# First attention in two PSUM banks, second attention's scores in two banks by turns

## The reference, cut to what matters

```python
x = x + tanh(g_xattn[0]) * xattn0(layernorm(x), ctx, mask)   # A: 4 heads of 64, one K/V head, rotary, masked, 120 context rows
x = x + tanh(g_ffn[0])   * ffn0(layernorm(x))                # F: gated SiLU, 704 wide, FP4 quantise-dequantise of inputs and weights
x = x + tanh(g_xattn[1]) * xattn1(layernorm(x), ctx, ctx)    # B: 16 heads of 16, biases, 120 context rows
x = x + tanh(g_ffn[1])   * moe(layernorm(x))                 # R, M: 8 experts, top 2, 1024 wide
```

## Time and profile before

| | us |
|---|---|
| median of 3 runs | 1848.67 |
| lowest, highest | 1848.36, 1865.61 |
| the profiled execution's own time | 1838.81 |
| span of its instructions | 1837.2 |
| TensorE busy | 1540.0 |
| VectorE busy | 1121.2 |
| ScalarE busy | 886.8 |
| GpSimd busy | 591.9 |

### The profile page before, as it was taken

One profiled execution on the slowest core, in us unless ns is written; L12 is line 12 of the kernel. 1 busy time (PEld: TensorE's weight loads), 2 busy tenths in 40 slices (PEclk: granted clock), 3 DMA queues, 4 the chain that ended last, 5 costly groups with the idle time before them and its releaser, 6 DMA issues.

```text
span 1837.2 us, 35831 instructions
## 1 busy us (share of the span) xinstructions
PE 1540.0 (84%) x12221; PEld 1239.6 (67%) x12222; DVE 1121.2 (61%) x2782; ACT 886.8 (48%) x2169; POOL 591.9 (32%) x704
## 2 busy tenths in 40 slices
PE   2334899999998999899989877649999999999994
PEld 1223577667766767676766554438888888888884
DVE  4657678877787778787777552234444444444442
ACT  1111466656666656665655453214444544445542
POOL 0002324333434243334332421023443434434432
PEclk9557999999999999999999896569999999999998
DMA  5002211222022202221122000157213232232224
GB/s 172 11 0 78 81 57 37 92 92 84 10 92 92 91 9 87 92 93 43 51 84 84 7 7 12 48 160 239 39 32 100 34 103 34 33 101 34 29 34 114
DMA packets 63088, 123.60 MB, mean 67 GB/s; under 512 B 13890, under 2 KB 51899, under 8 KB 58811
## 3 DMA queue, kind: packets, MB, share of 16 engines
q1 hardware_dynamic: 45675, 102.75, 16.3%
q0 software_dynamic: 17312, 19.56, 6.6%
HBM read 78.63 MB, written 48.04 MB: 69 GB/s over the span
## 4 chain that ended last, share of the span: by engine, by line
PE 76%; DVE 9%; ACT 7%; issue 3%; DMA 2%; POOL 1%; SPq 0%; ACTq 0%; DVEq 0%; POOLq 0%
PE bank L1247 17%; PE bank L1249 16%; PE bank L1248 16%; PE bank L1319 9%; PE bank L1343 7%; PE bank L1332 3%; ACT b_ex L687 2%; DVE b_mn L1008 2%; ACT b_q L747 1%; PE bank L1359 1%; PE bank L1521 1%; ACT r_z L670 1%; PE bank L1467 1%; PE bank L1411 1%; PE bank L1431 1%
## 5 line engine op out<-in xcount | busy, mean ns | idle before, releaser
L1247 PE MATMUL bank<-split_room,wm 128*128 128x256 f16 x1152 | 314.9, 273 | 8.3 <-issue 6.9
L1249 PE MATMUL bank<-split_room,wm 128*128 128x256 f16 x1152 | 314.8, 273 | 0.0
L1248 PE MATMUL bank<-split_room,wm 128*128 128x256 f16 x1152 | 314.7, 273 | 0.0
L1224 DVE SCALAR_TENSOR_TENSOR split_room<-bank,b12e,split_room 128x256 f32<-128x256 f32 x288 | 138.3, 484 | 266.0 <-ACT split_room L798 258.2
L798 ACT ACTIVATE split_room<-bank,b12e 128x256 f32<-128x256 f32 x288 | 134.3, 470 | 196.0 <-PE bank L1249 192.6
L687 ACT ACTIVATE b_ex<-bank,b_mn 128x120 f32<-128x120 f32 x512 | 143.6, 373 | 117.5 <-DVE b_mn L1008 116.4
L1319 PE MATMUL bank<-b_k,b_q 128*128 128x480 f32 x256 | 140.8, 634 | 39.0 <-ACT b_ex L687 23.3
L1343 PEld LDWEIGHTS bank<-b_v,b_pt 120*128 120x128 f32 x1024 | 137.9, 204 | 36.0 <-issue 31.7
L643 POOL DMA_INDIRECT acc<-split_room,m_cur x72 | 115.3, 1602 | 131.7 <-ACT split_room L812 104.3
L1247 PE MATMUL bank<-wm,split_room 128*128 128x256 f16 x576 | 157.0, 273 | 0.0
L1249 PE MATMUL bank<-wm,split_room 128*128 128x256 f16 x576 | 157.0, 273 | 0.0
(11 more groups left out here) (358 smaller groups left out, 3859.7 us busy)
## 6 DMA issues: line engine op xcount, KB each, us to landing
split_room<-in_L_ffn_W SPq DMA_DIRECT2D x48, 512.0 KB, 8.4
wsplit<-split_room SPq DMA_DIRECT2D x16, 1536.0 KB, 6.5
wm<-wsplit SPq DMA_DIRECT2D x16, 1536.0 KB, 8.9
acc<-x SPq DMA_DIRECT2D x17, 256.0 KB, 2.1
xin<-in_x SPq DMA_DIRECT2D x16, 256.0 KB
rows<-r_row SPq DMA_DIRECT2D x16, 256.0 KB, 8.2
ct<-in_ctx SPq DMA_DIRECT2D x16, 120.0 KB
cb<-in_ctx SPq DMA_DIRECT2D x16, 120.0 KB, 2.1
```

What stands on the lines that cost most here:

```text
L1224: dve.scalar_tensor_tensor(m_h[:, c % 3], bank[c % 4][:, TILE:2 * TILE], b12e[:, p, 1, c:c + 1], m_s[:, c % 2], ALU.add, ALU.mult).then_in ...
L1247: pe.matmul(o, lh, rh, start=start, stop=False)
L1248: pe.matmul(o, ll, rh, start=False, stop=False)
L1249: return pe.matmul(o, lh, rl, start=False, stop=stop)
```

## The change

- B's scores alternate between bank 3 and bank 2. Scores of round k wait for the exponentials of round k - 2, and the exponentials of round k from 2 on wait for the transposes of round k - 2, whose buffer they overwrite.
- A uses banks 0 and 1 alone. A.q is cut in two pieces, A.q0 and A.q1, one per pair of heads, each with both rotary halves in one bank (0 and 1); A.q1 waits until VectorE has read A.kv's results from bank 1. A.rot becomes A.rk (keys and values) and A.r0, A.r1 (queries, 256 wide each). A's values go into bank 0 for the first half of the queries and bank 1 for the second; the first wait until all of A's exponentials are done.
- B.q writes banks 3 and 2, and waits for the ranks no more; the first values of B wait for them instead.
- All five lists are new. The number and shape of products on TensorE are the same.

```diff
@@ -355,19 +355,19 @@
 
         RA, RB = NT, NT * (H1 // QUAD)
         ORDER = {
-            "SP": ("A.load/-1 B.out/3 B.load/0 W/0 R.rank/3").split(),
-            "POOL": ("B.ln/2 R.ln/3 A.ln/-1 F.p0/1 W0/0 W1/0 F.p1/1 F.ln/0 W2/0 F.p/0 R.scatter/3").split(),
-            "ACT": ("F.gu3/2 B.k/3 B.q/3 B.s0/3 B.s1/3 B.t0/3 F.ht0/2 B.s2/3 B.t1/3 B.t2/3 B.s3/3 F.ht1/2 A.s0/0 B.t3/3 "
-                "B.s4/3 B.s5/3 B.t4/3 F.z/1 A.s1/0 A.t0/0 B.s6/3 B.t5/3 A.t1/0 B.s7/3 B.t6/3 B.t7/3 F.t/1 A.ot/0 B.ot/3 "
-                "F.gu0/1 B.z/2 F.gu1/1 R.z/3 R.t/3 A.z/-1 B.ct/2 B.zt/2 F.gu2/1 A.t/-1 R.logit/3").split(),
-            "DVE": ("B.s0/3 F.q1b/2 B.v/3 B.s1/3 F.q1c/2 B.s2/3 F.ht0/2 A.rot/0 B.s3/3 A.s0/0 B.s4/3 F.ht1/2 F.ln/1 B.s5/3 "
-                "W0/1 A.s1/0 W1/1 B.s6/3 B.p3/3 F.q/1 B.s7/3 F.d1/2 A.p0/0 A.p1/0 F.t/1 B.p7/3 B.ln/2 A.ot/0 B.ot/3 W2/1 "
-                "B.out/3 F.gu0/1 R.ln/3 A.out/0 A.ln/-1 F.gu1/1 R.t/3 F.q0a/1 F.gu2/1 B.ct/2 R.logit/3 B.zt/2 R.rank/3 "
-                "A.t/-1 F.gu3/1 F.q0b/1 F.q1a/1 F.q0c/1").split(),
-            "PE": ("F.ht1/2 A.s0/0 B.t3/3 B.s4/3 B.p2/3 A.s1/0 A.t0/0 B.s5/3 B.t4/3 F.d0/2 B.s6/3 B.p3/3 F.d1/2 B.p4/3 "
-                "B.t5/3 B.s7/3 A.t1/0 A.p0/0 B.t6/3 B.p5/3 A.p1/0 B.t7/3 F.t/1 B.p6/3 B.p7/3 A.ot/0 B.ot/3 F.gu0/1 "
-                "B.out/3 A.out/0 F.gu1/1 B.ct/2 B.zt/2 R.t/3 F.gu2/1 R.logit/3 A.t/-1 F.gu3/1 R.rank/3 B.k/2 B.q/2 "
-                "A.kv/-1 B.s0/2 B.v/2 A.q/-1 B.s1/2 B.t0/2 F.ht0/1 B.s2/2 B.p0/2 B.t1/2 B.t2/2 B.s3/2 B.p1/2").split(),
+            "SP": ("A.load/-1 W/1 B.out/3 B.load/0 R.rank/3").split(),
+            "POOL": ("B.ln/2 A.ln/-1 R.ln/3 W0/1 F.p0/1 F.p1/1 W1/1 F.ln/0 F.p/0 W2/1 R.scatter/3").split(),
+            "ACT": ("B.s0/3 B.s1/3 B.t0/3 B.s2/3 B.t1/3 F.ht0/2 B.t2/3 B.s3/3 B.t3/3 F.ht1/2 B.s4/3 B.s5/3 F.z/1 B.t4/3 "
+                "A.s0/0 B.s6/3 B.t5/3 A.s1/0 A.t0/0 A.t1/0 B.s7/3 B.t6/3 F.t/1 A.ot/0 B.t7/3 F.gu0/1 B.ot/3 B.z/2 F.gu1/1 "
+                "A.z/-1 F.gu2/1 B.ct/2 B.zt/2 A.t/-1 F.gu3/1 R.z/3 R.t/3 B.k/2 B.q/2 R.logit/3").split(),
+            "DVE": ("B.s3/3 F.ht0/2 A.rk/0 A.r0/0 B.s4/3 F.ht1/2 F.ln/1 A.r1/0 B.s5/3 B.s6/3 B.p3/3 A.s0/0 F.q/1 B.s7/3 "
+                "A.s1/0 W0/2 F.d1/2 W1/2 A.p0/0 A.p1/0 F.t/1 A.ot/0 W2/2 B.p7/3 B.ln/2 F.gu0/1 A.out/0 B.ot/3 A.ln/-1 "
+                "F.gu1/1 B.out/3 F.q0a/1 F.gu2/1 R.ln/3 B.ct/2 B.zt/2 A.t/-1 F.gu3/1 F.q0b/1 R.t/3 F.q1a/1 F.q0c/1 "
+                "R.logit/3 B.s0/2 B.v/2 B.s1/2 R.rank/3 B.s2/2 F.q1b/1 F.q1c/1").split(),
+            "PE": ("F.ht1/2 A.q1/0 B.p2/3 B.s5/3 B.t4/3 B.s6/3 B.p3/3 A.s0/0 F.d0/2 A.s1/0 A.t0/0 B.p4/3 B.t5/3 B.s7/3 "
+                "F.d1/2 B.t6/3 B.p5/3 A.t1/0 A.p0/0 F.t/1 A.p1/0 B.t7/3 B.p6/3 A.ot/0 F.gu0/1 B.p7/3 A.out/0 B.ot/3 "
+                "F.gu1/1 B.out/3 F.gu2/1 B.ct/2 B.zt/2 A.t/-1 F.gu3/1 B.k/2 R.t/3 B.q/2 R.logit/3 B.s0/2 B.v/2 B.s1/2 "
+                "R.rank/3 A.kv/-1 B.t0/2 B.s2/2 B.p0/2 B.t1/2 F.ht0/1 B.t2/2 B.s3/2 B.p1/2 A.q0/-1 B.t3/2 B.s4/2").split(),
         }
         LAGS = [int(entry.split("/")[1]) for order in ORDER.values() for entry in order]
@@ -679,10 +679,13 @@
                 held(act, A.ct, b + 1)
                 act.activation(a_ct[:, 0].rearrange("p k t -> p (k t)"), bank[1][:, 0:NK * S], ACT.Copy).then_inc(A.ct_hi, 1)
 
-            def rounds(G, n, ex, sb_, mn, pt, tb):
+            def rounds(G, n, ex, sbs, mn, pt, tb):
                 def exps(k):
                     def stage(b, p):
                         held(act, G.mn, b * n + k + 1)
+                        if k >= 2:
+                            act.wait_ge(G.pt_mm, b * n + k - 1)
+                        sb_ = sbs[k % len(sbs)]
                         for h in range(QUAD):
                             last = act.activation(ex[:, k % 2, h], sb_[:, h * S:(h + 1) * S], ACT.Exp,
                                                   bias=mn[:, k % 2, h:h + 1], scale=-1.0)
@@ -697,8 +700,8 @@
 
                 return by_round(G, n, s=exps, t=turned)
 
-            ra = rounds(A, RA, a_ex, bank[0], a_mn, a_pt, bank[1])
-            rb = rounds(B, RB, b_ex, bank[3], b_mn, b_pt, bank[4])
+            ra = rounds(A, RA, a_ex, bank[0:1], a_mn, a_pt, bank[1])
+            rb = rounds(B, RB, b_ex, (bank[3], bank[2]), b_mn, b_pt, bank[4])
 
             def out_t(G, ot, bk):
                 def stage(b, p):
@@ -743,7 +746,7 @@
             def b_q_(b, p):
                 held(act, B.q_mm, b + 1)
                 for c in range(QUAD):
-                    src = bank[3 + 2 * (c // 2)][:, (c % 2) * T:(c % 2 + 1) * T]
+                    src = bank[3 - c // 2][:, (c % 2) * T:(c % 2 + 1) * T]
                     last = act.activation(b_q[:, c], src, ACT.Identity, bias=bqk[:, c:c + 1])
                 last.then_inc(B.q, 1)
...
@@ -978,33 +981,35 @@
                 low(flat(a_zt[:, 1]), bank[0][:, :], flat(a_zt[:, 0]), A.zt_hi, A.zt_lo, b + 1)
                 low(flat(a_ct[:, 1]), bank[1][:, 0:NK * S], flat(a_ct[:, 0]), A.ct_hi, A.ct_lo, b + 1)
 
-            def a_rotary(b, p):
+            def a_rotary_k(b, p):
                 ca.go_on(b)
-
-                def table(at, n, reps):
-                    return C[:, at:at + n].unsqueeze(1).to_broadcast([P, reps, n])
-                dve.wait_ge(A.q_mm, b + 1)
-                ca.link(dve.tensor_tensor(a_t1[:, :, :], bank[0][:, :].rearrange("p (c t) -> p c t", c=2), table(C_CQ, T, 2), ALU.mult))
-                ca.link(dve.tensor_tensor(a_t2[:, :, :], bank[2][:, :].rearrange("p (c t) -> p c t", c=2), table(C_SQ, T, 2), ALU.mult))
                 dve.wait_ge(A.kv_mm, b + 1)
                 ca.link(dve.tensor_tensor(a_k1[:, :], bank[1][:, 0:S], C[:, C_CK:C_CK + S], ALU.mult))
                 ca.link(dve.tensor_tensor(a_k2[:, :], bank[1][:, S:2 * S], C[:, C_SK:C_SK + S], ALU.mult))
                 dve.tensor_copy(a_v[:, 0:K0], bank[1][0:S, 2 * S:2 * S + K0]).then_inc(A.v, 1)
-                ca.wait(ca.n - 2)
-                dve.tensor_tensor(a_q[:, :, :], a_t1[:, :, :], a_t2[:, :, :], ALU.add).then_inc(A.q, 1)
                 ca.wait()
                 for j in range(2):
                     h = slice(K0 * j, K0 * (j + 1))
                     last = dve.tensor_tensor(a_k[h, j], a_k1[h, :], a_k2[h, :], ALU.add)
                 last.then_inc(A.k, 1)
 
-            def rounds(G, n, sbk, pbk, mn, rd, o, heads, width):
+            def a_rotary(c):
+                def stage(b, p):
+                    ca.go_on(b)
+                    dve.wait_ge(A.q_mm, b * 2 + c + 1)
+                    ca.link(dve.tensor_tensor(a_t1[:, c], bank[c][:, 0:T], C[:, C_CQ:C_CQ + T], ALU.mult))
+                    ca.link(dve.tensor_tensor(a_t2[:, c], bank[c][:, T:2 * T], C[:, C_SQ:C_SQ + T], ALU.mult))
+                    ca.wait()
+                    dve.tensor_tensor(a_q[:, c], a_t1[:, c], a_t2[:, c], ALU.add).then_inc(A.q, 1)
+                return stage
+
+            def rounds(G, n, sbks, pbks, mn, rd, o, heads, width):
                 per = n // NT
 
                 def minima(k):
                     def stage(b, p):
                         dve.wait_ge(G.s_mm, b * n + k + 1)
-                        s4 = sbk[:, 0:QUAD * S].rearrange("p (h s) -> p h s", h=QUAD)
+                        s4 = sbks[k % len(sbks)][:, 0:QUAD * S].rearrange("p (h s) -> p h s", h=QUAD)
                         dve.tensor_reduce(mn[:, k % 2], s4, AX.X, ALU.min).then_inc(G.mn, 1)
                     return stage
@@ -1012,7 +1017,7 @@
                     def stage(b, p):
                         t = k // per
                         dve.wait_ge(G.pv_mm, b * NT + t + 1)
-                        pv = pbk[:, 0:heads * (width + 1)].rearrange("p (h d) -> p h d", h=heads)
+                        pv = pbks[t][:, 0:heads * (width + 1)].rearrange("p (h d) -> p h d", h=heads)
                         dve.reciprocal(rd[:, t], pv[:, :, width]).then_inc(G.rd, 1)
                         dve.wait_ge(G.rd, b * NT + t + 1)
                         dve.tensor_tensor(o[:, t].rearrange("p (h d) -> p h d", h=heads), pv[:, :, 0:width],
@@ -1023,8 +1028,8 @@
                 made.update({f"{G.name}.p{k}": values(k) for k in range(per - 1, n, per)})
                 return made
 
-            ra = rounds(A, RA, bank[0], bank[2], a_mn, a_rd, a_o, H0, K0)
-            rb = rounds(B, RB, bank[3], bank[5], b_mn, b_rd, b_o, H1, K1)
+            ra = rounds(A, RA, bank[0:1], bank[0:2], a_mn, a_rd, a_o, H0, K0)
+            rb = rounds(B, RB, (bank[3], bank[2]), (bank[5], bank[5]), b_mn, b_rd, b_o, H1, K1)
 
             def out_t(G, ot, bk):
                 def stage(b, p):
...
@@ -1275,15 +1280,18 @@
                 pe.wait_ge((B.c_in0, B.c_in1)[p], (b - p) * 8 + 16)
                 c_t(B, cb[:, p], bank[4])
 
-            def a_q_(b, p):
-                pe.wait_ge(A.zt_lo, b + 1)
-                pe.wait_ge(wA_done, 1)
-                for w, bk in ((wqa, bank[0]), (wqb, bank[2])):
-                    for c in range(2):
+            def a_q_(c):
```

(38 more changed lines are left out.)

2 lines of the change are left out of this document (1 added, 1 removed).

## The result

The changed kernel takes 1763.88 us (median of four runs, 1761.78 to 1765.24) against 1848.51 us for the kernel before beside it (1834.79 to 1865.61): a ratio of 0.957 over the single runs (the two medians alone give 0.954), with a 95% interval of 0.951 to 0.962. The profiled execution took 1764.79 us, its span is 1763.1; before it was 1838.81 and 1837.2.

What follows compares the result with a forecast made beforehand. TensorE, busy 92% of a 60.1 us step, bounds the kernel, with 4.9 us waiting. Thirteen steps at 2.2 us (28.6) plus 12 in the drain give 40.6: 1808 from the median, 1798 profiled; forecast 1785 to 1828, wider range 1776 to 1850.

Steps and rivals of the forecast that it cites:

- The full step: Steps between rank products: 60.1 us with 4.9 of TensorE waits, forecast to become 57.9 by saving 2.2 a step.
- The walked waits: TensorE's waits left in one full step traced stage by stage: together 2.7 us against 4.9 before.
- The drain: Last 190.5 us, where the second attention's chain stands bare: at most 15.6 us to gain, 12 taken.
- The single covers: Drain waits hidden by other work: logits cover nearly all of b_q's 5.2 us, keys remove 3.5 of r_z's.
- Rival 4: Drain: denser rounds keep TensorE at 2.4 GHz, up to 34 us to win, half giving 1790, down to 1770; chance 0.10.
- ScalarE's tables: Table loads on ScalarE: four a step become two, giving back 2.6 us a step, off TensorE's path.
- The rotation in halves: VectorE: three 512-wide instructions become six of 256, adding 0.8 us a step (between 0 and 2.0), covered by idle time.
- The weights: Weight loads, now on SP ahead of B.out: 8.4 us to landing, hidden as the copy is needed about 15 us later.
- Warm-up: The time before the first b_q at 222.7 us: forecast gain 0.
- 1 (the waits only move): Full steps: other waits replace those removed, bringing the step back to 59.6 us; 1836, range 1830 to 1850; chance 0.19.
- 2 (VectorE bound at F.gu1): VectorE's late gate product delays F.gu1; decides from 2.2 us on, at 4.7 the kernel takes 1869; chance 0.10.
- 3 (alternating banks shake the clock): Full steps: cycling banks bring a tenth of them to 1.2 GHz, adding 72 us, 1880 in all; chance 0.06.

## Why the prediction was right and wrong

**The full step** (57.9 us forecast, 57.62 measured) was right, and as to TensorE's waits for its reasons. The walked waits of 0.9, 0.7, 0.45, 0.35 and 0.3 came out as 0.75 (F.gu1), 0.75 (a_ex), 0.20 (b_q), 0.53 (the transposes behind b_pt, 5.8 / 11) and none (F.gu3). Their sum is 2.41 with the two small rows, for 2.7. Of the 7.6 us by which the thirteen steps came out better than the forecast 28.6, 3.0 lie in the eleven steps of the window (27.2 for 11 x 2.2), and 4.6 in the first and the last, which fell from 123.0 to 114.0 us together and which I had priced like the rest.

**The drain is the term that failed,** and in it the step that took TensorE's busy time as fixed: 12 us forecast, 35.8 measured. Of it 18.8 is idle time and 15.7 busy time up to the last rank product, 1.3 comes after. The single covers were good: the r_z wait lost 3.5 (forecast 3.5), b_q 4.8 (nearly all of 5.2). The attentions' waits lost 10.2 where I had 7.0, because a bare round needs less idling than walked (9.4 us left for 12.6). Then I took 12 of the 15.6 because part of the drain "runs at half clock"; that was wrong in kind. The clock is not a reason to discount a saved wait, it adds to it: with fewer waits the granted clock of this stretch went from 0.75 to 0.84, and the products that stayed took 15.7 us less. The feeding of the old drain bears out that the clock there follows the idling (0.75 to 0.88 with useless work, and a shorter drain, in one trace of each). By changes, the banks with the old orders gave 18.1 us of the drain, and the loads that the change removed there are worth 6.6 in the new order; the other 11 belong to the orders or to how the parts work together. Rival 4 had the clock as a case of its own, half of 34 us for it, with a chance of 0.10. The size of that came out close (15.7 for 17), though its case ended at 1770 and the time is 1764; and its chance was too small, for it was no alternative to the forecast but a part of it.

**ScalarE's tables.** Two loads a step, as forecast. That they are "off TensorE's path" fell: put back in the new order they cost 3.1 us a step and, those that the change removed from it, 6.6 in the drain; in the old order, taken away, they bring nothing. The walked step did have ScalarE with two loads in it, so the sentence was wrong and the sum held only because the walk had them gone. The Trainium skill (ScalarE: Activation LUTs, What ACT_TABLE_LOAD costs) has 2.66 us for a change of tables. The timeline has the activation 0.01 us behind the load of 1.28; no second half is seen in any run here. An estimate by that page would make the two loads 5.3 us of ScalarE. By the rows they are 2.6, and of the 3.1 that they cost the step 1.3 are waits and 1.8 TensorE's busy time at the lower clock.

**The rotation in halves.** Six of 0.42 us against three of 0.67 is 0.5 a step, forecast 0.8, and it lies beside other work. Missed was another of VectorE's costs, below, 1.3 us a step, also covered. **The weights** stayed hidden: no row of TensorE's full steps waits for them. **Warm-up** gained 3.2 us that I had at nothing; where, I did not examine.

**The rivals.** 1 (the waits only move) is refuted for the change and is what the old orders with the new banks did. 2 (VectorE bound at F.gu1): the wait is there, 0.75, and never reached the 2.2 from which it decides. 3 (alternating banks shake the clock) is refuted at its size: the changed kernel's full steps ran at 0.98 against 0.99, with eight short stretches at 1.2 GHz in 600 us against three (and seven where the same old instructions ran at 0.96), and the single bank in the same orders is at 0.91. The Trainium skill's rule (TensorE: Matmul & The Clock Gate, A second HAM failure mode: psum-queue depth-cycling) would have the two-bank kernel as the one that swings; here it is the one-bank kernel.

**The base.** The profiled execution of before was 9.7 us under its median of 1848.5, the changed one 0.9 over its own. The gain in the medians, 84.6 us, is therefore 10.6 more than the 74.0 between the profiles. It belongs to the spread of the kernel before (its medians over the comparisons lie between 1825.8 and 1848.5), which the changed one hardly shows (1763.9, 1761.1 and 1765.0).

**Open.** What decides the half-clock stretches in full steps. With 6.8 us of idling a step the old orders with new banks ran at 1.00, and with less the kernels with fewer and with more table loads ran at 0.96 and 0.95; the same instructions ran at 0.99 in one execution and at 0.96 in another. How much of the drain's 15.7 us comes from which wait was not separated. The old drain without added products was traced once, so how much its length differs between executions isn't known.

## What to carry to other kernels

Price a saved wait twice where TensorE's clock is already low: once as time, and once as the clock that it gives back to the work around it. A second buffer and the order that uses it are one change; half of it can cost more than the whole brings, so test them together. A stage that looks cheap on an engine with idle time is on the path as soon as its queue holds the next exponentials behind it.
